# A second cross attention whose maxima are turned by DMA and whose last key group uses float32 values

## The reference

```python
q = (query @ Wq + bq).reshape(b, sq, 16, 64)
k = (key @ Wk + bk).reshape(b, 4096, 16, 64)
v = (value @ Wv + bv).reshape(b, 4096, 16, 64)
attn = jax.nn.softmax(jnp.einsum('bqhd,bkhd->bhqk', q, k) / 8, axis=-1)
out = jnp.einsum('bhqk,bkhd->bqhd', attn, v).reshape(b, sq, 1024)
out = out @ Wo + bo + residual      # then a layer norm
```

## Time and profile before

| | us |
|---|---|
| median of three runs | 1978.18 |
| the three runs | 1962.81, 1978.18, 1979.93 |
| the profiled execution | 1967.77 |
| its span in the profile | 1965.9 |
| busy in it: PE, DVE, ACT, Pool | 1636.9, 1261.0, 984.0, 668.2 |

### The profile page before, as it was taken

The page is one execution under the profiler, slowest core; times in us unless marked ns, Lnnn a source line. Parts: engine busy times, 40 slices in busy tenths (PEclk is TensorE's granted clock), DMA queues, the critical chain, the costliest instruction groups (busy, mean ns, idle before and its releaser), DMA issues. The chain is left out here.

```text
span 1965.9 us, 52765 instructions
## 1 busy us (share of the span) xinstructions
PE 1636.9 (83%) x20036; PEld 961.1 (49%) x20036; DVE 1261.0 (64%) x1971; ACT 984.0 (50%) x1591; POOL 668.2 (34%) x499
## 2 busy tenths in 40 slices
PE   4999999995999999989677368888888888876672
PEld 2445545451334343345433137777776776743442
DVE  3666666554999999836585266666666666236946
ACT  2555555551787878836300135555555555515621
POOL 2330000001111111103210048888888888703400
PEclk8999999996899999985688679999999999887686
DMA  4698979885322222130000715544554543120000
GB/s 158 186 220 236 226 216 223 234 201 143 93 65 66 65 66 65 43 144 1 1 1 1 240 32 140 137 133 131 133 132 125 138 117 94 32 89 1 1 0 11
DMA packets 171211, 213.32 MB, mean 109 GB/s; under 512 B 49928, under 2 KB 144532, under 8 KB 166446
## 3 DMA queue, kind: packets, MB, share of 16 engines
q1 hardware_dynamic: 169776, 210.48, 39.6%
q10 hardware_dynamic: 1280, 0.53, 0.1%
HBM read 123.37 MB, written 87.57 MB: 107 GB/s over the span
## 5 line engine op out<-in xcount | busy, mean ns | idle before, releaser
L1084 POOL TENSOR_TENSOR x_r<-x_p 128x1024 f16<-128x1024 f32 x256 | 477.1, 1893 | 101.9 <-ACT x_p L1056 101.5
L1102 DVE TENSOR_REDUCE x_mx<-a_all 128x2 f32<-128x1024 f32 x256 | 313.4, 1224 | 197.6 <-PE a_all L955 197.6
L1056 ACT ACTIVATE x_p<-s_all 128x1024 f32<-128x1024 f32 x256 | 258.4, 1020 | 139.5 <-PE s_all L939 136.6
L717 ACT ACTIVATE x_p<-s_all 128x1024 f32<-128x1024 f32 x256 | 261.1, 1023 | 49.2 <-PE s_all L627 42.0
L772 DVE TENSOR_REDUCE x_mx<-a_all 128x1 f32<-128x512 f32 x352 | 229.4, 681 | 17.2 <-PE o_all L638 8.8
L986 PE MATMUL o_all<-x_v,x_p 64*128 64x129 f16 x4096 | 218.9, 218 | 11.7 <-issue 8.7
L939 PE MATMUL s_all<-x_q,x_k 64*128 64x256 f16 x3072 | 216.4, 271 | 9.6 <-issue 9.6
L990 PE MATMUL o_all<-x_v,x_r 64*128 64x65 f16 x4096 | 211.6, 190 | 0.6 <-issue 0.6
L986 PEld LDWEIGHTS o_all<-x_v,x_p 64*128 64x128 bf16 x4096 | 192.8, 94 | 22.9 <-issue 17.7
L990 PEld LDWEIGHTS o_all<-x_v,x_r 64*128 64x128 f16 x4096 | 185.9, 95 | 18.6 <-issue 1.3
L939 PEld LDWEIGHTS s_all<-x_q,x_k 64*128 64x128 f16 x3072 | 160.0, 95 | 49.7 <-issue 14.0
(11 more groups left out here) (333 smaller groups left out, 3212.9 us busy)
## 6 DMA issues: line engine op xcount, KB each, us to landing
values<-vst SPq DMA_DIRECT2D x16, 2064.0 KB, 10.6
x_v<-values SPq DMA_DIRECT2D x32, 1032.0 KB, 5.1
keys<-kst SPq DMA_DIRECT2D x32, 1024.0 KB, 7.0
x_k<-keys SPq DMA_DIRECT2D x128, 256.0 KB, 4.6
x_k<-keys SPq DMA_DIRECT2D x192, 64.0 KB, 2.1
values<-vst SPq DMA_DIRECT2D x16, 528.0 KB, 12.8
x_v<-values SPq DMA_DIRECT2D x32, 264.0 KB, 2.6
cf<-in_ctxT SPq DMA_DIRECT2D x16, 512.0 KB, 9.6
```

The lines of the kernel that those rows point to most:

```text
L717: act.activation(prob[g % NP][:], chip.s_ps[g % 2][:].rearrange("p (c q) -> p c q", q=SQ), ACT.Exp, scale=hd ** -0.5).then_inc(p_ready, 1)
L1056: act.activation(prob[g % NP][:], chip.s_ps[g % 2][:].rearrange("p (c q) -> p c q", q=SQ), ACT.Exp, scale=hd ** -0.5).then_inc(p_ready, 1)
L1084: pool.tensor_tensor(rest[g % NP][:], prob[g % NP][:], hi, ALU.subtract).then_inc(rest_done, 1)
L1102: dve.tensor_reduce(mx[a[1] % 2][:, n // 4, 2 * (n % 4):2 * (n % 4) + 2], chip.a_all[:, :].rearrange("p (h c) -> p h c", h=2), AX.X, ALU.m ...
```

## The change

**Queries.** `project_queries` loses its bias and its `early`. The second layer has its own `project_queries_wide`. The keys of unit 0 are issued in the layer norm's block. The halves `qh` and `ql` now belong to the buffers of the attention and outlive the block. Tile 0, which holds the heads of the first four units, is written and read back at once; the seven others are written behind the loads, and SP waits for them only in the next block, ahead of its first reload. ACT no longer reads queries.

```diff
+            def _(sp):
+                sp.dma_start(bq[:], bias_q).then_inc(loaded, 16)
+                qd = buffers.q_dram.rearrange("h (m p) t -> h p m t", p=P)
+                sp.wait_ge(hi, 1)
+                sp.dma_start(qd[0, :, 0], qh[:, 0, :]).then_inc(buffers.first_written, 16)
+                sp.wait_ge(lo, 1)
+                sp.dma_start(qd[1, :, 0], ql[:, 0, :]).then_inc(buffers.first_written, 16)
+                buffers.load_keys(sp, 0, 1)
+                sp.wait_ge(buffers.first_written, 32)
+                for u in range(4):
+                    buffers.load_queries(sp, 0, u)
+                buffers.load_values(sp, 0, 0)
+                for u in range(2, 4):
+                    buffers.load_keys(sp, 0, u)
+                    buffers.load_values(sp, 0, u - 1)
+                buffers.load_values(sp, 0, 3)
+                sp.wait_ge(hi, MT)
+                sp.dma_start(qd[0, :, 1:], qh[:, 1:, :]).then_inc(buffers.written, 16)
+                sp.wait_ge(lo, MT)
+                sp.dma_start(qd[1, :, 1:], ql[:, 1:, :]).then_inc(buffers.written, 16)
```

```diff
-                def maximum_columns(a):
+                def turn(a):
                     i = a[1] % 2
                     act.wait_ge(nm_done, nth(a, 1, 1))
-                    act.activation(mcol[i][:, :, :, 0], nm[i][:].unsqueeze(2).to_broadcast([P, 2, 2]), ACT.Copy).then_inc(mcol_done, 1)
-
-                def queries(a):
-                    act.wait_ge(qm_ready, nth(a, 1, 1))
-                    act.activation(qm[a[1] % 2][:], chip.a_all[:, 0:SQ], ACT.Copy).then_inc(qm_done, 1)
+                    for h in range(2):
+                        for t in range(2):
+                            act.dma_start(qm[i][64 * h:64 * h + 1, t * P:(t + 1) * P], nm[i][:, t:t + 1]).then_inc(qm_turned, 8 * 2)
```

```diff
+        def chunk_banks(u, g):
+            return chip.o_all if not real(u) and g % 2 else chip.a_all
...
-                    if real(u) or g + 8 * u[1] > -14:
+                    into = chunk_banks(u, g)
+                    if real(u):
                         pe.wait_ge(pair_done, nth(u, GR, 14 + g))
-                    if g == 5 and (real(u) or u[1] == -1):
-                        pe.wait_ge(qm_done, nth(u, 1, 2))
+                    elif g + 8 * u[1] > -13:
+                        pe.wait_ge(pair_done, nth(u, GR, 13 + g))
...
-                        if g == 4 and (real(u) or u[1] == -1) and ahead(u, 1):
-                            negated_maxima(u, ahead(u, 1))
+                        elif u[1] == -1 and g in (5, 6):
+                            scores((0, 0), g - 5)
```

```diff
+                            if g == GR - 1:
+                                for h in range(2):
+                                    r = slice(64 * h, 64 * h + 64)
+                                    last = pe.matmul(chip.o_ps[h][:, qt * VC:qt * VC + 1 + hd], prob[i][r, c, qs], vs[w % 2][r, c, :],
+                                                     start=False, stop=c == GK - 1 and qt == 1, skip_group_check=True)
+                                continue
...
+                    w = u[1]
+                    pool.wait_ge(v_loaded[w], u[0] * 16 + 16)
+                    if not (number(u) is not None and number(u) < 2):
+                        pool.wait_ge(pv_done, nth(u, GR, -GR))
                     for g in range(GR):
+                        if g == GR - 1:
+                            vd = v[w][:].rearrange("p (h c) e -> p h c e", h=2)[:, :, SK // 2 // P - 2:, :]
+                            pool.tensor_tensor(vs[w % 2][:, :, 1:].rearrange("p (h c) e -> p h c e", h=2), vd[:, :, :, 1:1 + hd], vd[:, :, :, 1 + hd:],
+                                               ALU.add).then_inc(rest_done, 1)
+                            continue
```

More of the change, by code:

```diff
@@ L401, in _, with project_queries @@
                 step(PAIRS - 1, 1, True)
-def project_queries(chip, tag, weight, bias_q, hd, q_dram, early=None):
+def project_queries(chip, tag, weight, hd, q_dram):
     nc = chip.nc
@@ L410, in project_queries @@
         w = weight.w
-        bq = chip.sb(f"{tag}_bq", [P, MT], F32, scope)
         qh = chip.sb(f"{tag}_qh", [P, MT, TOK], F16, scope)
         ql = chip.sb(f"{tag}_ql", [P, MT, TOK], F16, scope)
-        loaded, ready, hi, lo, out = (chip.sem(f"{tag}_{n}") for n in ("ld", "rdy", "hi", "lo", "out"))
+        ready, hi, lo, out = (chip.sem(f"{tag}_{n}") for n in ("rdy", "hi", "lo", "out"))
         with nc.Block() as block:
@@ L417, in _ @@
             def _(sp):
-                if bias_q is not None:
-                    sp.dma_start(bq[:], bias_q).then_inc(loaded, 16)
-                if early is not None:
-                    early(sp)
                 qd = q_dram.rearrange("h (m p) t -> h p m t", p=P)
@@ L816, in __init__, with loads @@
         self.v_loaded = [chip.sem(f"{tag}_vld{w}") for w in range(4)]
+        self.qh = chip.sb(f"{tag}_qh", [P, NH * 64 // P, TOK], F16, scope)
+        self.ql = chip.sb(f"{tag}_ql", [P, NH * 64 // P, TOK], F16, scope)
+        self.first_written, self.written = chip.sem(f"{tag}_qw0"), chip.sem(f"{tag}_qw")
+    def loads(self, sp):
+        self.load_keys(sp, 0, 0)
     def load_keys(self, eng, it, w):
@@ L835, in load_values, with project_queries_wide, _ @@
         eng.dma_start(self.v[w][:], vd.rearrange("h p c e -> p (h c) e")).then_inc(self.v_loaded[w], 16)
+def project_queries_wide(chip, tag, weight, bias_q, buffers):
+    nc = chip.nc
+    MT = NH * 64 // P
+    with ExitStack() as scope:
+        w, qh, ql = weight.w, buffers.qh, buffers.ql
+        bq = chip.sb(f"{tag}_bq", [P, MT], F32, scope)
+        loaded, ready, hi, lo = (chip.sem(f"{tag}_{n}") for n in ("ld", "rdy", "hi", "lo"))
+        with nc.Block() as block:
+            @block.sync
+            def _(sp):
[18 more added lines that the diff above has]
+                sp.dma_start(qd[1, :, 1:], ql[:, 1:, :]).then_inc(buffers.written, 16)
+            @block.tensor
+            def _(pe):
+                pe.wait_ge(weight.loaded, 16)
+                for m in range(MT):
+                    if m >= 4:
+                        pe.wait_ge(lo, m - 3)
+                    for k in range(KT):
+                        last = pe.matmul(chip.banks[m % 4], w[:, k, m * P:(m + 1) * P], chip.xnT[:, k, :],
+                                         start=(k == 0), stop=(k == KT - 1))
+                    last.then_inc(ready, 1)
+            @block.scalar
+            def _(act):
+                act.wait_ge(loaded, 16)
+                for m in range(MT):
+                    act.wait_ge(ready, m + 1)
+                    act.activation(qh[:, m, :], chip.banks[m % 4], ACT.Identity, bias=bq[:, m:m + 1]).then_inc(hi, 1)
+            @block.vector
+            def _(dve):
+                for m in range(MT):
+                    dve.wait_ge(hi, m + 1)
+                    dve.scalar_tensor_tensor(out=ql[:, m, :], in0=chip.banks[m % 4], scalar=bq[:, m:m + 1],
+                                             in1=qh[:, m, :], op0=ALU.add, op1=ALU.subtract).then_inc(lo, 1)
@@ L1048, in body @@
                             act.wait_ge(cleared, 2)
-                            maximum_columns((0, 0))
-                            queries((0, 0))
+                            turn((0, 0))
                         return
@@ L1060, in body @@
                         if g == 3 and ahead(u, 1):
-                            maximum_columns(ahead(u, 1))
-                        if g == 6 and ahead(u, 1):
-                            queries(ahead(u, 1))
+                            turn(ahead(u, 1))
                         if g == 7 and ahead(u, -1):
@@ L1073, in _ @@
                 for i in range(2):
-                    pool.memset(mcol[i][:], 0.0).then_inc(cleared, 1)
+                    pool.memset(qm[i][:], 0.0).then_inc(cleared, 1)
+                for i in range(2):
+                    pool.memset(vs[i][:, :, 0:1], 1.0).then_inc(cleared, 1)
+                pool.wait_ge(cleared, 4)
                 def body(u):
```

66 lines of the change are left out of this document (18 added, 48 removed).

## The result

The changed kernel takes 2001.82 us (median of 4 runs, 1999.53 to 2008.58), the kernel before, run beside it, 1977.24: a ratio of 1.0146, 95% interval 1.0099 to 1.0193. It is slower by 1.5%, which is outside the forecast range of 1944 to 2000. The profiled execution took 2003.68 us with a span of 2001.9, 36.0 above the span of before. That splits by starts of rows: up to the layer norm ahead of the projection 11.2 us less (1069.10 against 1080.30; nothing was changed there, and over all profiled executions of this study this time lies between 1068.7 and 1081.3, in no order by kernel; why was not looked into, and it is not counted to the change), from there to the first exp 12.3 less (61.6 against 73.9), over the exps 60.9 more, behind them 1.4 less. So the question is one of 61 us in the steady part, where the forecast had 21, and of 12 us in the prologue, where it had 20.

What follows compares the result with a forecast made beforehand. In the second cross attention, PE's own pace plus waits set the 17.05 us unit, after a start waiting for DMAs. Steady part plus 21 us and prologue minus 20 gave plus 1 us: 1969 us, range 1944 to 2000.

Steps and rivals of the forecast that it cites:

- float32 values: Group 7's values as 16 float32 products, row halves side by side: 1.78 us, plus 1.08 us per unit.
- rival 2: Group 7: load and matmul don't overlap within a half; step 2.8 us, kernel 1983 us; chance 8%.
- rival 3: Group 7: the two halves load one after the other; step 3.57 us, kernel 2004 us; chance 6%.
- Negated maxima: Between scores of groups 6 and 7: PE's two products and the wait ahead of them go, minus 1.02 us per unit.
- The turn: Four DMAs on ACT after exp 3 delay the output copy that group 0's values await: plus 0.6 us per unit.
- T: Time ACT takes to issue the four DMAs that turn the maxima: 2.2 us, ends 1.0 and 7.9.
- The issue gaps: Steady part: PE pauses with no wait the profile shows, about 1.1 us per unit, covering some of the copy wait.
- Pool: Per unit, Pool loses a subtraction and gains a smaller sum: falls to 13.8 us, not the bound, nothing gained.
- The prologue: Before the first exp: earlier loads, faster first chunk maxima; first exp at 1134.5 against 1154.2, minus 20 us.
- rival 5: Prologue: the last query write holds SP to 1122, so the prologue gives 14 us; kernel 1975 us; chance 10%.
- sign of a wrong prologue: A first exp after 1140 us would make the prologue forecast wrong.
- The sum: Whole kernel: steady part plus 21 us (1.08 - 1.02 + 0.6, times 32), prologue minus 20: plus 1 us.

Runs made afterwards that it cites:

- e2: The kernel before with only the float32 values step of group 7 and Pool's sum added: 2009.76 us (1.0176).
- e4: The changed kernel with the maxima turned by two DMAs per unit in place of four: 1985.76 us (1.0057).
- e1: The changed kernel without the float32 step, group 7's values again in half precision: 2013.69 us (1.0194).
- e5: The changed kernel with the maxima turned by eight DMAs per unit in place of four, each row in two halves: 2118.11 us (1.0766).
- e8: The kernel before with 128 satisfied waits ahead of PE's loop and nothing else: 1949.65 us (0.9915).
- e17: The changed kernel with 384 satisfied waits ahead of PE's loop: 2045.92 us, a single execution.
- e18: New prologue alone, 128 waits ending the projection's PE work, loads of values 0 to 3 and keys 2 and 3 behind the last query writes: 1924.01 us (0.9744).

## Why the prediction was wrong

- *float32 values.* Forecast 1.78 us for the step and plus 1.08 per unit; the row shows 32 matmuls within 1.90 us and S4 to S5 grew by 0.98 (e2: 1.04). Right. (16 loads of 0.110 us are 1.76, not 1.78; that is 0.6 us in the sum.) The Trainium skill ("TensorE: Matmul & The Clock Gate", The mechanism) has a load overlap matmuls only across row groups, which gave rival 2's 2.8 us; the trace does not bear this out, nor rival 3's 3.57.
- *Negated maxima.* Forecast minus 1.02 per unit; S6 to S7 went from 2.74 to 1.85, to 1.78 in e4. Right within 0.1.
- *The turn.* Forecast T = 2.2 us and a wait of 0.7 us in the mean; measured 2.43 to 3.68 us per four (median 0.62 each) and 25.4 us in all, 0.8 per unit; S5 to S6 grew by 0.90 where the term had 0.6. The mechanism was right (e1, e4, e5), the size low by some 10 us over 32 units. In the mean of the four places the wait is 37.4 us, 1.2 per unit, and the growth 1.28, twice the term. Nearer rows stood in the trace of before: SP's own batches of four query reads in the attention, of which the timeline shows 27, took 2.40 to 3.39 us, all above T. One is

```profile
1394.32 2.40 SPq L829 DMA_DIRECT2D x_q<-queries  x4
```

- *The issue gaps.* This is the step that failed: "The rest, about 1.1 us per unit, is issue" was carried over unchanged, and even used as cover for the wait. The pauses grew by 16.1 us, and the scores behind them run at the half clock, so that with S1 to S4 (7.71 against 6.81 us) 29 us came in where the sum had nothing. e8 to e17 show that such pauses move with the place of the loop's code while its work stays the same, and that of the 29 us the means over four places keep 3. That the growth at no shift is therefore one of place, and not of the edits, is the likeliest reading, not a shown one. What a pause itself is stays open. From the trace of before alone their size after any edit of PE's stream could not be known; what the forecast lacked was their range, for the kernel before 20 us down to 49 us up with the same work, in place of zero.
- *Pool* did not bind: right, 13.9 against 13.8 us.
- *The prologue.* Forecast minus 20, measured minus 12.3. The pairs went 1.13 us apart (forecast 1.28), the start was the error: the last query write stood 8.82 us behind the loads, so the block ended at 1111.4, which counted as in the trace of before (11.2 later) is 1122.6, the 1122 of rival 5 and not the 1116 of the forecast. The first exp, counted so, is at 1141.9 against 1134.5, past the 1140 that the forecast had named as its sign of a wrong prologue. e18 shows the cause by putting the write ahead of the loads. The bound was in the text; I gave it 10% although the row of before showed the same write standing 11.45 us.
- *The sum.* Terms as measured: 31 (float32) - 28 (S6 to S7) + 29 (S5 to S6) + 29 (S1 to S4) = 61, which is what was seen, and minus 12 for the prologue. The forecast had 35 - 33 + 19 + 0 and minus 20. As an estimate free of place the change costs some 37 - 12 = 25 us, with the 37 anywhere from 10 to 61 by the four differences; "about no change" was then too kind by the wait for the copy and the prologue alone.

## What to carry to other kernels

Two edits that each lengthen another engine's path to the same meeting point do not add: measure each alone before keeping the pair, since here the float32 step was nearly free only in front of a wait that the other edit had made. Count DMA issues on a busy engine as work of that engine (0.6 us each here), and put the one that a block's end depends on ahead of bulk loads. Where a long unrolled loop shows "issue" pauses at its back edge, time the kernel at several places of its code before a difference of a few per cent is put down to an edit.

## What the runs showed of the hardware that I had not expected

- PE's pauses in a loop of four unrolled units depend on where the loop's code lies: 19.5 to 65.7 us in all for the same work, back to the start at a shift of 256 instructions (29.5 against 33.4 us). In the trace of before the instruction queue moves 2.10 MB in 128 packets, 16.4 KB each. That a packet holds about 256 instructions, and that the pauses are waits for such packets, is a guess from these two figures; no run shows it.
- Behind the longer pauses at the back edge (5.00 us in the row shown) the scores run at 1.2 GHz, 0.61 in place of 0.39 us. So such a pause costs more than its length: S2 to S3 is then about 3.1 us in place of 1.79, the next scores starting at 1308.81 in the row's unit.
- The median time of an issue goes by the DMA and not by its packets: with 128 of two bytes, 128 of four or 64 of two it is 0.62, 0.59 and 0.62 us of ACT. The longest ones are 1.87, 0.63 and 1.80 us.
